# Mamba stage of a four-layer chain: three state buffers, softplus and first products moved, norm rows and residual on ScalarE and GpSimd

## The chip, the cores and the metric

The kernel runs on one core of a Trainium2 chip. The metric is the time of one execution in device microseconds; a median over runs is given. The engines are TensorE (PE in the rows, PEld is its weight load), VectorE (DVE), ScalarE (ACT), GpSimd (POOL) and SyncE (SP), which issues all transfers here.

## The reference

Four blocks follow one another on x of shape (4, 512, 256), in float32: two cross-attention blocks, a Mamba block and a last attention block. Only the Mamba block (the middle stage) is touched. It works on sequences of 64 context rows followed by 512 rows, for 4 batches, in 4 layers:

```python
def mamba_block(x, ip_w, cw, cb, xp_w, dtp_w, dtp_b, A_log, Dp, op_w):
    xz = jnp.einsum('bsd,ed->bse', x, ip_w)
    xi, z = jnp.split(xz, 2, axis=-1)
    ...
    xi = jax.nn.silu(conv.transpose(0, 2, 1))
    xdbl = jnp.einsum('bse,fe->bsf', xi, xp_w)
    dt, Bm, Cm = jnp.split(xdbl, [DR_, DR_ + DS_], axis=-1)
    dt = jax.nn.softplus(jnp.einsum('bsr,er->bse', dt, dtp_w) + dtp_b)
    A = -jnp.exp(A_log)
    dA = jnp.exp(dt[..., None] * A)
    dBu = dt[..., None] * Bm[:, :, None, :] * xi[..., None]
    ...            # h = dA * h + dBu ; y = sum over states of h * C
    y = ys.transpose(1, 0, 2) + xi * Dp
    y = y * jax.nn.silu(z)
    return jnp.einsum('bse,de->bsd', y, op_w)
...
h = h + mamba_block(rmsnorm(h, norm_w[l]), ...)    # for each of 4 layers
```

The inner width is 512, there are 16 states, a convolution over 4 rows, and rmsnorm is x * rsqrt(mean(x*x) + eps) * w.

## The kernel before, in words

The Mamba stage holds everything feature-major: 128 features by columns, where the columns are the 4 batches of 576 rows laid end to end. They are cut into five chunks (`CHUNKS`) of 384, 512, 512, 512 and 384 columns. One chunk of one layer is an item, `g` from 0 to 19; items 0, 5, 10, 15 are the first of a layer and 4, 9, 14, 19 the last (`last_of`).

An item is 64 units: 16 states `n` by 4 feature tiles `e`, numbered `q = 4n + e`. In each unit ScalarE computes a decay exp(dt*A) into one of three PSUM banks (L1800, `decay`, two units ahead of the scan), GpSimd multiplies u by the B row into one of four buffers `db` (L2052, `state_input`, three units ahead), and VectorE runs the recurrence as one scan instruction (L2004) into the state buffer `hh`, of which there are two, picked by `n % 2`. After the four scans of a state TensorE transposes them in tiles of 128 rows (`turn`, L1729). Of a 512-wide item two of the four tiles go to bank 5 (`TURN_D`), where VectorE multiplies each with its C column and adds it to `yt` (L2018; for state 0 a plain product, L2014). The other two go to bank 6 (`TURN_P`), where ScalarE scales them into `ys` (`scaled`, L1812) and TensorE adds them up with an identity product (`add`, L1739). ScalarE also keeps the last column of each state for the next item (`keep`, L1821), and a scan into a state buffer waits for the `keep` and the last turn of the state that was in it.

Between the units stand the side jobs of the two neighbouring items (`side`): those of the item before, `post` (back-turn of y, gating, output product, residual into `h`), and those that prepare the next, `pre` (norm, input products, convolution, x and dt products, softplus, gate z). At which unit each stands is set by a table of numbers:

```python
VAR, IN, YF, CONV, XD = 1, (6, 8, 10, 12), (14, 16, 18, 20), (22, 25, 28, 31), 34
DTP, BCT, SOFT, OUT, Z = 37, 44, 45, (58, 61), (46, 49, 52, 55)
```

The numbers are the units at which TensorE does its part; ScalarE and VectorE follow one to three units later. Every engine takes its instructions strictly in this written order. All side products go through a single PSUM bank, 7 (`SIDES`), so each waits until the one before it has been emptied. So at the start of an item (q = 0) ScalarE squares h (L1847); at q = 2 it turns the mean into rstd with a logarithm and an exponential (L1852, L1855), each of which is preceded by a table load; at q = 4 and 5 VectorE makes the normed rows `xn` (L1962); and from q = 6 TensorE makes the input products from them, which ScalarE copies into `xc` (L1862) and SyncE writes to memory for the convolution. VectorE adds the two halves of the output product to `h` at q = 60 and 63 (L1948).

## Time and profile before

| | |
|---|---|
| median of 3 runs | 4411.18 us (4409.15 to 4416.01) |
| the profiled execution's own time | 4420.25 us |
| its span in the trace | 4418.1 us |
| busy, of the span: TensorE, VectorE, ScalarE, GpSimd | 85%, 69%, 53%, 48% |
| Mamba stage, first to last scan | 1501 to 3590 us, 2089 us |

Busy shares of the whole span mix stages; the Mamba stage is read by itself. In the rows below, consecutive instructions of one engine overlap by some 0.09 us: two scans in a row are given as 2.45 us while one is 1.27 us, so the step from start to start is what an instruction costs.

### The profile page before, as it was taken

How to read it: one execution, taken by the hardware profiler on the slowest of the kernel's cores; microseconds unless marked ns; L12 is line 12 of the kernel's file. 1: busy time of each engine (PE TensorE's matmuls, PEld its weight loads, DVE VectorE, ACT ScalarE, POOL GpSimd, SP SyncE). 2: the span in 40 equal slices, each digit the busy share in tenths (PEclk: the TensorE clock that was granted, in tenths of full speed). 3: DMA queues.
4: the chain of work that ended last, by engine and by line, in shares of the span. 5: the costliest groups of instructions: out<-in, count | busy, mean ns of one | idle time of the engine just before them, and what ended most of it. 6: DMA issues, size and time to landing. Idle time of an engine off the chain costs nothing. (4 is left out here: it accounts for less than half of the span.)

```text
span 4418.1 us, 51543 instructions
## 1 busy us (share of the span) xinstructions
PE 3755.0 (85%) x16536; PEld 1943.5 (44%) x16536; DVE 3056.4 (69%) x4176; ACT 2354.4 (53%) x4473; POOL 2114.1 (48%) x2144
## 2 busy tenths in 40 slices
PE   8999999999988688888888888887888768888787
PEld 4444444444444244444444444444444434344443
DVE  4426435364353499999999999999999956474653
ACT  2334323233231477767777677776777626354462
POOL 1003112031120378877888877787788833132230
PEclk9999999999999799999999999999999979999999
DMA  3110000000000533223332233322432120000000
GB/s 147 39 57 1 1 19 1 10 10 1 15 1 0 150 84 87 75 81 94 91 87 72 78 94 87 86 83 78 112 87 80 46 79 1 11 1 11 1 6 5
DMA packets 135961, 228.47 MB, mean 52 GB/s; under 512 B 19280, under 2 KB 118864, under 8 KB 126864
## 3 DMA queue, kind: packets, MB, share of 16 engines
q1 hardware_dynamic: 135696, 225.20, 17.3%
q8 instruction: 135, 2.21, 0.2%
q14 instruction: 130, 1.06, 0.1%
HBM read 192.55 MB, written 32.60 MB: 51 GB/s over the span
## 5 line engine op out<-in xcount | busy, mean ns | idle before, releaser
L2052 POOL TENSOR_TENSOR m_db<-m_u,m_bb 128x512 f32<-128x512 f32 (+1 forms) x1280 | 1466.1, 1165 | 418.6 <-DVE m_hh L2004 415.4
L2004 DVE TENSOR_TENSOR_SCAN m_hh<-psum,m_kept,m_db 128x512 f32<-128x512 f32 (+1 forms) x1024 | 1196.2, 1202 | 29.9 <-ACT m_kept L1821 23.3
L1800 ACT ACTIVATE psum<-m_dt,m_am 128x512 f32<-128x512 f32 (+1 forms) x1280 | 817.7, 644 | 394.2 <-DVE m_hh L2004 390.6
L1729 PE MATMUL psum<-cst,m_hh 128*128 128x128 f32 x4608 | 659.7, 284 | 324.8 <-DVE m_yt L2018 227.6
L1729 PEld LDWEIGHTS psum<-cst,m_hh 128*128 128x128 f32 x4608 | 524.3, 144 | 753.4 <-DVE m_yt L2018 440.1
L1739 PE MATMUL psum<-m_ys,cst 128*128 128x512 f32 x1024 | 545.5, 615 | 0.0
L2018 DVE SCALAR_TENSOR_TENSOR m_yt<-psum,m_bc,m_yt 128x512 f32<-128x512 f32 x600 | 437.9, 730 | 41.1 <-PE psum L1729 40.0
L798 POOL TENSOR_SCALAR a_pr<-a_pr,a_ri 128x512 f32<-128x512 f32 x256 | 174.1, 694 | 609.5 <-DVE a_ri L612 609.5
L1812 ACT ACTIVATE m_ys<-psum,m_bc 128x512 f32<-128x512 f32 x512 | 344.7, 673 | 25.5 <-PE psum L1729 24.0
L798 POOL TENSOR_SCALAR c_pr<-c_pr,c_ri 128x512 f32<-128x512 f32 x256 | 172.5, 694 | 364.6 <-DVE c_ri L731 364.6
L652 ACT ACTIVATE a_pr<-psum,a_mx 128x512 f32<-128x512 f32 x256 | 173.7, 684 | 268.2 <-DVE a_mx L602 268.2
L1615 PE MATMUL psum<-m_xn,m_wa 128*128 128x512 f32 (+1 forms) x640 | 296.7, 591 | 3.9 <-DVE m_xn L1962 3.6
L2004 DVE TENSOR_TENSOR_SCAN m_hh<-psum,m_db 128x384 f32<-128x384 f32 x256 | 232.4, 941 | 19.9 <-ACT m_kept L1821 11.7
L602 DVE TENSOR_REDUCE a_mx<-psum 128x2 f32<-128x1024 f32 x128 | 155.9, 1220 | 130.4 <-PE psum L552 130.4
L1739 PEld LDWEIGHTS psum<-m_ys,cst 128*128 128x128 f32 x1024 | 170.0, 196 | 97.6 <-issue 71.7
L723 DVE TENSOR_REDUCE c_mx<-psum 128x1 f32<-128x512 f32 x256 | 164.0, 683 | 59.3 <-PE psum L679 59.3
L787 ACT ACTIVATE c_pr<-psum,c_mx 128x512 f32<-128x512 f32 x256 | 173.3, 684 | 49.9 <-DVE c_mx L723 48.7
L532 POOL TENSOR_TENSOR a_pr<-a_pr,a_ri 128x512 f32<-128x512 f32 x32 | 33.3, 1042 | 292.6 <-DVE a_ri L498 292.6
L688 PE MATMUL psum<-cst,c_pr 128*128 128x128 f32 x1024 | 156.4, 288 | 19.8 <-ACT c_ptr L773 15.3
L562 PE MATMUL psum<-cst,a_pr 128*128 128x128 f32 x1024 | 153.2, 284 | 18.2 <-POOL a_pr L798 15.9
L562 PEld LDWEIGHTS psum<-cst,a_pr 128*128 128x128 f32 x1024 | 111.4, 143 | 128.4 <-DVE a_slots L635 64.5
L635 DVE COPY a_slots<-psum 128x512 f32<-128x512 f32 x256 | 162.7, 676 | 6.8 <-PE psum L562 6.8
(242 smaller groups left out, 5624.2 us busy)
## 6 DMA issues: line engine op xcount, KB each, us to landing
m_bb<-b_rows SPq DMA_DIRECT2D x48, 1024.0 KB, 4.7
m_xr<-x_line SPq DMA_DIRECT2D x128, 192.0 KB, 4.0
m_bb<-b_rows SPq DMA_DIRECT2D x32, 768.0 KB, 4.5
m_xr<-x_line SPq DMA_DIRECT2D x128, 160.0 KB, 3.6
m_xr<-x_line SPq DMA_DIRECT2D x128, 128.0 KB, 3.3
m_xr<-x_line SPq DMA_DIRECT2D x128, 96.0 KB, 3.5
x_line<-m_xc SPq DMA_DIRECT2D x32, 192.0 KB, 2.8
m_wa<-w_in SPq DMA_DIRECT2D x4, 1376.0 KB, 7.4
```

The source lines that it names most:

```text
L562: mm = nc.tensor.transpose(b[:, kt * P:(kt + 1) * P], self.pr[:, u % 6, kt * P:(kt + 1) * P], ident)
L652: nc.scalar.activation(self.pr[:, u % 6, :], self.full(f"{name} s {u}"), ACT.Exp, bias=self.nm[:, u % 8:u % 8 + 1], accum_out=self.smh[:, ...
L787: nc.scalar.activation(self.pr[:, u % 6, :], self.full(f"{name} s {u}"), ACT.Exp, bias=self.nm[:, u % 8:u % 8 + 1], accum_out=self.smh[:, ...
L798: nc.gpsimd.tensor_scalar(self.pr[:, u % 6, :], self.pr[:, u % 6, :], self.rih[:, u % 8:u % 8 + 1], 1.0, ALU.mult, ALU.mult)\
L1615: mm = nc.tensor.matmul(full(job)[0:m, 0:w], lhs, rhs, start=k == 0, stop=k == n - 1)
L1729: mm = nc.tensor.transpose(s[:, e * P:(e + 1) * P], hh[:, n % 2, e, t * P:(t + 1) * P], ident)
L1739: nc.tensor.matmul(bank(SUMS[k]), ident, ys[:, k, :], start=n == 0, stop=n == LAST)\
L1800: nc.scalar.activation(bank(DECAY[u % len(DECAY)])[:, 0:w], dt[:, g % 2, e, 0:w], ACT.Exp, scale=am[:, layer_of(g) % 2, e * DS + n:e * DS ...
L1812: nc.scalar.activation(ys[:, k, :], bank(TURN_P), ACT.Identity, scale=bc[:, g % 2, t, DR + DS + n:DR + DS + n + 1], bias=0.0)\
L2004: nc.vector.tensor_tensor_scan(hh[:, n % 2, e, 0:w], bank(DECAY[u % len(DECAY)])[:, 0:w], db[:, u % 4, 0:w], kept[:, n, e:e + 1] if g % NI ...
L2018: nc.vector.scalar_tensor_tensor(y, bank(TURN_D), c, y, ALU.mult, ALU.add)\
L2052: nc.gpsimd.tensor_tensor(db[:, u % 4, 0:w], us[:, g % 2, e, 0:w], bb[:, at % 2, n % 4, 0:w], ALU.mult).then_inc(pool_done, pr.pool.step(f ...
```

## The change

It has seven parts.

1. `hh` gets three buffers, picked by `(16g + n) % 3`. To make room, `xc` now shares the memory of `yg`, and `sq` that of a new `res`, which brings new waits.
2. Softplus moves from unit 45 to 46; the gate products Z from 46, 49, 52, 55 to 47, 50, 53, 55; the products u on GpSimd from 50, 52, 54, 56 to 51, 53, 55, 57.
3. The first products of each item (state 0, two tiles) go from VectorE to ScalarE (`first`).
4. The normed rows: ScalarE multiplies h by the weight right after the squares (`weighted`, two instructions), and GpSimd multiplies that by rstd at q = 5 and 6; VectorE's two instructions are gone.
5. The input products move from 6, 8, 10, 12 to 7, 9, 11, 13.
6. The residual: ScalarE takes the output product out of PSUM, halved (`res`), and GpSimd adds it to `h`; VectorE's two instructions are gone. The output products move from 58, 61 to 57, 60.
7. The small vectors are loaded ahead of the weights, with a semaphore of their own (`vectors_loaded`).

```diff
@@ tables and buffers
-            hh = sb("hh", [P, 2, NE, BANK])
+            HH = 3
+            hh = sb("hh", [P, HH, NE, BANK])
+            rstd = sb("rstd", [P, BANK])
+            res = sb("res", [P, ND, BANK])
+            sq = res
             yg = sb("yg", [P, NE, BANK])
+            xc = yg
-            VAR, IN, YF, CONV, XD = 1, (6, 8, 10, 12), (14, 16, 18, 20), (22, 25, 28, 31), 34
-            DTP, BCT, SOFT, OUT, Z = 37, 44, 45, (58, 61), (46, 49, 52, 55)
+            VAR, IN, YF, CONV, XD = 1, (7, 9, 11, 13), (14, 16, 18, 20), (22, 25, 28, 31), 34
+            DTP, BCT, SOFT, OUT, Z = 37, 44, 46, (57, 60), (47, 50, 53, 55)
+            U, CUT = (51, 53, 55, 57), 58
@@ ScalarE
+                    def first(g, k):
+                        t = tiles_d(g)[k]
+                        if k == 0 and g >= 2:
+                            act.wait_ge(pe_done, pr.pe.at(f"{g - 2} yf {NE - 1}"))
+                        act.wait_ge(pe_done, pr.pe.at(f"{g} ht 0 {t}"))
+                        nc.scalar.activation(yt[:, g % 2, t, :], bank(TURN_D), ACT.Identity,
+                                             scale=bc[:, g % 2, t, DR + DS:DR + DS + 1], bias=0.0)\
+                            .then_inc(act_done, pr.act.step(f"{g} y 0 {t}"))
...
+                            for j in range(ND):
+                                if q == OUT[j] + 2:
+                                    if post:
+                                        act.wait_ge(pool_done, pr.pool.at(f"{post - 1} h {j}"))
+                                    act.wait_ge(pe_done, pr.pe.at(f"{post} out {j}"))
+                                    nc.scalar.activation(res[:, j, 0:width(post)], full(f"{post} out {j}")[:, 0:width(post)],
+                                                         ACT.Copy, scale=0.5).then_inc(act_done, pr.act.step(f"{post} res {j}"))
...
+                            if g >= 3:
+                                act.wait_ge(pool_done, pr.pool.at(f"{g - 3} h 1"))
                             for j in range(ND):
                                 nc.scalar.activation(sq[:, j, 0:w], h[:, j, at:at + w], ACT.Square)\
                                     .then_inc(act_done, pr.act.step(f"{g} squares" if j else None))
+                            act.wait_ge(vectors_loaded, 16 * (layer_of(g) + 1))
+                            for j in range(ND):
+                                nc.scalar.activation(xn[:, j, 0:w], h[:, j, at:at + w], ACT.Copy, scale=vec2(g, "norm", j))\
+                                    .then_inc(act_done, pr.act.step(f"{g} weighted" if j else None))
...
-                            nc.scalar.activation(s, s, ACT.Exp, scale=-0.5)\
+                            nc.scalar.activation(rstd[:, 0:w], s, ACT.Exp, scale=-0.5)\
                                 .then_inc(act_done, pr.act.step(f"{g} rstd"))
...
                             if before and e == 1:
+                                if before[1] == 0:
+                                    first(before[0], 0)
                                 scaled(*before, 0)
...
+                                if before[1] == 0:
+                                    first(before[0], 1)
@@ VectorE
+                                    if post + 2 < ITEMS:
+                                        dve.wait_ge(x_written[e % 2], written(post + 2, e))
                                     nc.vector.scalar_tensor_tensor(yg[:, e, 0:w], xi[:, post % 2, e, 0:w],
...
-                                if q == OUT[j] + 2:
-                                    dve.wait_ge(pe_done, pr.pe.at(f"{post} out {j}"))
-                                    nc.vector.scalar_tensor_tensor(h[:, j, at:at + w], full(f"{post} out {j}")[:, 0:w], 0.5,
...
-                            if q == VAR + 3 + k:
-                                dve.wait_ge(act_done, pr.act.at(f"{g} rstd"))
...
-                                nc.vector.scalar_tensor_tensor(xn[:, k, 0:w], h[:, k, at:at + w], vec2(g, "norm", k),
-                                                               full(f"{g} var")[:, 0:w], ALU.mult, ALU.mult)\
...
-                            if DS * g + n >= 2:
-                                i, m = divmod(DS * g + n - 2, DS)
+                            if DS * g + n >= HH:
+                                i, m = divmod(DS * g + n - HH, DS)
@@ GpSimd
+                                if q == OUT[j] + 3:
+                                    pool.wait_ge(act_done, pr.act.at(f"{post} res {j}"))
+                                    nc.gpsimd.tensor_tensor(h[:, j, at:at + w], h[:, j, at:at + w], res[:, j, 0:w], ALU.add)\
+                                        .then_inc(pool_done, pr.pool.step(f"{post} h {j}"))
...
+                            if q == VAR + 4 + k:
+                                pool.wait_ge(act_done, pr.act.at(f"{g} rstd"))
+                                nc.gpsimd.tensor_tensor(xn[:, k, 0:w], xn[:, k, 0:w], rstd[:, 0:w], ALU.mult)\
+                                    .then_inc(pool_done, pr.pool.step(f"{g} xn" if k else None))
```

ScalarE, around the start of item 12 (q = 63 of item 11 to q = 2), before: decay, the two squares, decay, scaled tile, decay, keep, then the logarithm and the exponential with their table loads.

```order
L1800 ACTIVATE psum<-m_dt,m_am 128x512
L1847 ACTIVATE m_sq<-m_h 128x512 x2
L1800 ACTIVATE psum<-m_dt,m_am 128x512
L1812 ACTIVATE m_ys<-psum,m_bc 128x512
L1800 ACTIVATE psum<-m_dt,m_am 128x512
L1821 ACTIVATE m_kept<-m_hh 128x4
L1852 ACT_TABLE_LOAD
L1852 ACTIVATE psum<-psum,m_eps 128x512
L1855 ACT_TABLE_LOAD
L1855 ACTIVATE psum<-psum 128x512
```

The same place of the change (the squares are written into `res`, L1874; the weighted rows are L1878, the residual copy L1856):

```order
L1856 ACTIVATE m_res<-psum 128x384
L1808 ACTIVATE psum<-m_dt,m_am 128x512
L1820 ACTIVATE m_ys<-psum,m_bc 128x512
L1808 ACTIVATE psum<-m_dt,m_am 128x512
L1874 ACTIVATE m_res<-m_h 128x512 x2
L1878 ACTIVATE m_xn<-m_h,m_va 128x512 x2
L1808 ACTIVATE psum<-m_dt,m_am 128x512
L1820 ACTIVATE m_ys<-psum,m_bc 128x512
L1808 ACTIVATE psum<-m_dt,m_am 128x512
L1839 ACTIVATE m_kept<-m_hh 128x4
L1883 ACT_TABLE_LOAD
L1883 ACTIVATE psum<-psum,m_eps 128x512
```

The second half of the residual copy stands three activations ahead of the squares, and two weighted rows now stand between the squares and the next decay.

ScalarE a little later (q = 4 to 6 of item 12), before, from the first `yp` copy (L1831) on:

```order
L1831 ACTIVATE m_yp<-psum 128x512
L1800 ACTIVATE psum<-m_dt,m_am 128x512
L1812 ACTIVATE m_ys<-psum,m_bc 128x512
L1800 ACTIVATE psum<-m_dt,m_am 128x512
L1821 ACTIVATE m_kept<-m_hh 128x4
```

And of the change, where the first product is L1830:

```order
L1849 ACTIVATE m_yp<-psum 128x512
L1808 ACTIVATE psum<-m_dt,m_am 128x512
L1830 ACTIVATE m_yt<-psum,m_bc 128x512
L1820 ACTIVATE m_ys<-psum,m_bc 128x512
L1808 ACTIVATE psum<-m_dt,m_am 128x512
L1839 ACTIVATE m_kept<-m_hh 128x4
```

The first product stands ahead of the scaled tile of state 0.

TensorE from the last gate product (`m_xn`, q = 55) to the last half of the output product (`m_yg`) in item 11, before; `m_hh` x8 are two turns of four transposes, `m_ys` the identity product of the sum:

```order
L1615 MATMUL psum<-m_xn,m_wa 128x512 x2
L1729 MATMUL psum<-cst,m_hh 128x128 x8
L1739 MATMUL psum<-m_ys,cst 128x512
L1729 MATMUL psum<-cst,m_hh 128x128 x8
L1615 MATMUL psum<-m_yg,m_wb 128x384 x2
L1739 MATMUL psum<-m_ys,cst 128x512
L1615 MATMUL psum<-m_yg,m_wb 128x384 x2
L1729 MATMUL psum<-cst,m_hh 128x128 x8
L1739 MATMUL psum<-m_ys,cst 128x512
L1615 MATMUL psum<-m_yg,m_wb 128x384 x2
L1729 MATMUL psum<-cst,m_hh 128x128 x8
L1615 MATMUL psum<-m_yg,m_wb 128x384 x2
```

And of the change:

```order
L1623 MATMUL psum<-m_xn,m_wa 128x512 x2
L1737 MATMUL psum<-cst,m_hh 128x128 x8
L1747 MATMUL psum<-m_ys,cst 128x512
L1623 MATMUL psum<-m_yg,m_wb 128x384 x2
L1737 MATMUL psum<-cst,m_hh 128x128 x8
L1623 MATMUL psum<-m_yg,m_wb 128x384 x2
L1747 MATMUL psum<-m_ys,cst 128x512
L1737 MATMUL psum<-cst,m_hh 128x128 x8
L1623 MATMUL psum<-m_yg,m_wb 128x384 x2
L1747 MATMUL psum<-m_ys,cst 128x512
L1623 MATMUL psum<-m_yg,m_wb 128x384 x2
L1737 MATMUL psum<-cst,m_hh 128x128 x8
```

The last half of the output product now stands ahead of the turns of q = 62, where it stood behind them.

## Rows read from the trace of the kernel before

**Rows 1.** The page, part 1: busy time of each engine, share of the span, instructions.
```profile
PE 3755.0 (85%) x16536; PEld 1943.5 (44%) x16536; DVE 3056.4 (69%) x4176; ACT 2354.4 (53%) x4473; POOL 2114.1 (48%) x2144
```

**Rows 2.** Windows: us, busy PE, PEld, DVE, ACT, POOL, PEclk; Mamba stage, then item 11.
```profile
1501.00:3590.00 2089.00, 1752.43 (x7889) 948.21 (x7887) 1975.55 (x2259) 1509.85 (x2648) 1647.45 (x1500) 0.96 0.30 84
2641.20:2753.20 112.00, 97.26 (x431) 51.85 (x430) 106.63 (x115) 83.20 (x143) 89.32 (x74) 0.95 0.31 90
```

**Rows 3.** Groups by line, 1501:3590, VectorE: xcount | busy us, mean ns | idle before.
```profile
L2004 DVE TENSOR_TENSOR_SCAN m_hh<-psum,m_kept,m_db 128x512 f32<-128x512 f32 (+1 forms) x1024 | 1196.2, 1202 | 29.9 <-ACT m_kept L1821 23.3 <-ACT psum L1800 5.1 <-POOL m_db L2052 1.4
...
L2018 DVE SCALAR_TENSOR_TENSOR m_yt<-psum,m_bc,m_yt 128x512 f32<-128x512 f32 x600 | 437.9, 730 | 41.1 <-PE psum L1729 40.0
...
L2014 DVE TENSOR_SCALAR m_yt<-psum,m_bc 128x512 f32<-128x512 f32 x40 | 29.1, 728 | 0.1
...
L1962 DVE SCALAR_TENSOR_TENSOR m_xn<-m_h,m_va,psum 128x512 f32<-128x512 f32 (+1 forms) x38 | 26.3, 692 | 6.0 <-ACT psum L1855 6.0
...
L1948 DVE SCALAR_TENSOR_TENSOR m_h<-psum,m_h 128x512 f32<-128x512 f32 (+1 forms) x38 | 24.2, 638 | 16.1 <-PE psum L1615 16.1
```

**Rows 4.** The same view, 1501:3590, GpSimd and ScalarE.
```profile
L2052 POOL TENSOR_TENSOR m_db<-m_u,m_bb 128x512 f32<-128x512 f32 (+1 forms) x1279 | 1465.1, 1165 | 418.6 <-DVE m_hh L2004 415.4 <-DVE m_cwr L1971 1.6 <-POOL m_db L2052 0.3
...
L1812 ACT ACTIVATE m_ys<-psum,m_bc 128x512 f32<-128x512 f32 x512 | 344.7, 673 | 25.5 <-PE psum L1729 24.0
```

**Rows 5.** Waits of VectorE, 1500:3750: us in total, times, longest.
```profile
DVE m_yt L2018 <- PE psum L1729: 40.0, 58, 2.3
DVE m_hh L2004 <- ACT m_kept L1821: 35.0, 16, 2.9
DVE m_h L1948 <- PE psum L1615: 26.4, 25, 7.9
```

**Rows 6.** Timeline of ScalarE, item 11, softplus: start, us, idle before in brackets.
```profile
2719.32 1.28 ACT L1892 ACT_TABLE_LOAD   x1
...
2723.84 0.69 ACT L1800 ACTIVATE psum<-m_dt,m_am 128x512 f32<-128x512 f32 x1
```

**Rows 7.** Timeline of VectorE, item 11, after the softplus.
```profile
2724.88 1.28 DVE L2004 TENSOR_TENSOR_SCAN m_hh<-psum,m_kept,m_db 128x512 f32<-128x512 f32 x1 [2.19 <-ACT m_kept L1821]
...
2728.80 2.45 DVE L2004 TENSOR_TENSOR_SCAN m_hh<-psum,m_kept,m_db 128x512 f32<-128x512 f32 x2
```

**Rows 8.** Timeline of TensorE, item 11, gate products to output products.
```profile
2727.25 3.57 PE L1615 MATMUL psum<-m_xn,m_wa 128*128 128x512 f32 x4
...
2737.92 1.98 PE L1615 MATMUL psum<-m_xn,m_wa 128*128 128x512 f32 x4
...
2750.86 1.46 PE L1615 MATMUL psum<-m_yg,m_wb 128*128 128x384 f32 x4
2752.15 1.02 PE L1739 MATMUL psum<-m_ys,cst 128*128 128x512 f32 x2
2753.01 1.04 PE L1729 MATMUL psum<-cst,m_hh 128*128 128x128 f32 x8
```

**Rows 9.** Timeline of ScalarE across the boundary from item 11 to item 12.
```profile
2752.88 1.14 ACT L1847 ACTIVATE m_sq<-m_h 128x512 f32<-128x512 f32 x2
2754.54 0.69 ACT L1800 ACTIVATE psum<-m_dt,m_am 128x512 f32<-128x512 f32 x1 [0.52 <-DVE m_hh L2004]
...
2756.57 1.28 ACT L1852 ACT_TABLE_LOAD   x1
...
2760.33 0.69 ACT L1800 ACTIVATE psum<-m_dt,m_am 128x512 f32<-128x512 f32 x1
...
2763.21 0.69 ACT L1812 ACTIVATE m_ys<-psum,m_bc 128x512 f32<-128x512 f32 x1
```

**Rows 10.** Timeline of TensorE, first units of item 12.
```profile
2761.67 1.11 PE L1729 MATMUL psum<-cst,m_hh 128*128 128x128 f32 x4 [1.62 <-ACT m_ys L1812]
...
2765.44 1.88 PE L1615 MATMUL psum<-m_xn,m_wa 128*128 128x512 f32 x4
```

**Rows 11.** Timeline of VectorE, item 12, tenth and eleventh unit.
```profile
2772.54 0.75 DVE L2018 SCALAR_TENSOR_TENSOR m_yt<-psum,m_bc,m_yt 128x512 f32<-128x512 f32 x1 [0.46 <-PE psum L1729]
```

More of the change, by code:

```diff
@@ L1440, in build @@
             h = sb("h", [P, ND, B * S2])
-            xc = sb("xc", [P, NE, BANK])
             xr = sb("xr", [P, 2, 4, BANK])
@@ L1921, in _ @@
                                 keep(*before)
-                            if before and e == 3 and len(tiles_p(before[0])) > 1:
-                                scaled(*before, 1)
+                            if before and e == 3:
+                                if len(tiles_p(before[0])) > 1:
+                                    scaled(*before, 1)
+                                if before[1] == 0:
+                                    first(before[0], 1)
                             side(NE * n + e, *neighbours(g))
@@ L2101, in prepare @@
                             rates(layer_of(g))
-                        if q == SOFT + 12 and border(g) is not None:
+                        if q == CUT and border(g) is not None:
                             b = border(g)
```

68 lines of the change are left out of this document (34 added, 34 removed).

## The prediction

> **What bounds the kernel now.** The page comes first, for the shares of the whole span [rows 1]. They mix four stages, and the change touches one, so the next view is the windows: in the Mamba stage VectorE is busy 1975.6 of 2089 us, GpSimd 1647, ScalarE 1510, TensorE 1752 [rows 2]. That says VectorE, and the waits agree: GpSimd's and ScalarE's largest idle is until a scan is done [rows 4], while VectorE's own waits are short. But 113 us of VectorE's stage are idle, and who ends these waits decides what less VectorE work is worth: TensorE's turns 40 us, ScalarE's `keep` 35 us, the output product 26 us [rows 5]. So the third view is the timeline of one item, read by units q. There VectorE is not alone on the path: TensorE is busy 97.3 of item 11's 112.0 us [rows 2], and around the start of an item ScalarE's chain of squares, logarithm, exponential and two table loads runs with all of its two-unit lead used up.
>
> **VectorE's side of the sum.** It loses 40 first products of 0.73 us, 38 normed rows of 0.69 and 38 residual additions of 0.64 [rows 3], busy 79.6 us. One instruction costs its length less an overlap of about 0.09 us (a pair of scans is 2.45 us long, one is 1.28 [rows 7]), so 116 of them free about 79.6 - 10 = 70 us. Beside it stand waits that could go: 35 us at `keep` and 26 us at the output product [rows 5]. If all of it came through, the kernel would be about 70 + 50 = 120 us faster. I don't think so, for what follows; the working is for item 11 and the start of item 12, whose rows are typical (the stage repeats itself by layers).
>
> **Softplus.** ScalarE starts its table load at 2719.32 and issues the next decay at 2723.84 [rows 6], 4.52 us, over twice its lead. VectorE waits 2.19 us, by the row for `keep` [rows 7]. A third state buffer takes the `keep` out of it, but that decay lasts until 2724.53, 0.35 us before the scan starts: alone it is worth 0.3 us. One unit later, softplus has one more decay ahead of it. The block ends 0.7 us later (a decay of 0.61 and a `keep`), and the scan that waits is the next one, at about 2724.95; with one gate row (0.58) then still to be done, the scan of unit 50 starts near 2727.7 instead of 2728.80 [rows 7]. After the second gate row the lead is 1.65 us. Call it 1.1 to 1.7 us an item.
>
> **From the gate to the output product.** What becomes of this lead is TensorE's to say. All side products pass through bank 7. The last gate product stays at unit 55, and it needs the gate row before it, which VectorE did at unit 54 and now does at 55, behind one more scan and one more addition (1.18 + 0.65 us). So the lead of 1.65 us is used up and the product starts at 2738.0, as before [rows 8]. Behind it TensorE has, in written order, this product 1.72, two turns 0.87 three times, the sum 0.86 three times, and four half output products of 1.29 each from start to start [rows 8]: 1.72 + 2.61 + 2.58 + 5.16 = 12.1 us, so the last half ends at 2750.1 where it ended at 2752.15. VectorE no longer waits for it (0.61 + 0.5 us twice at the wide ones, 0.46 at the narrow ones), but the turns of unit 62 now stand behind it and come 0.9 us later. Gain at the end of the item: about 1.9 us.
>
> **The start of the next item.** This is where I expect it to go. ScalarE takes the residual out of PSUM (0.5 us, to 2750.65), then come decay, scaled tile, decay (0.61 + 0.57 + 0.61) and the squares can start at 2752.5, against 2752.88 [rows 9]; GpSimd's addition, which they also wait for, is ready by then (a product is 1.17 us [rows 4]). Two weighted rows follow, priced as the two squares, 1.06 us. Of these 0.52 are covered, since the decay behind them waits that long for a scan today [rows 9]. So the logarithm starts 1.06 - 0.52 - 0.4 = 0.1 to 0.2 us later than now. From its table load to the next decay are 3.76 us (2756.57 to 2760.33 [rows 9]), and today scan 5 starts as that decay ends: the normed row that leaves VectorE there was filler, and so are most of the next three removed instructions, because the decays of units 5 to 9 come one by one behind it. Then the first product (0.57 us, priced as the scaled tile, 0.67 long [rows 4]) stands ahead of the scaled tile of state 0, which TensorE waits for (1.62 us for the one before it [rows 10]). Some 0.4 us of that is absorbed, for TensorE today starts the next turns 0.4 us after the tile is ready. The first input product thus comes 0.3 to 0.5 us later than at 2765.44 [rows 10], and from there to unit 15 TensorE has no idle time: a product 1.72, a sum 0.86 and two turns 0.87 are 3.45 us for two units, and VectorE needs 3.0. It waits for the turns already today (0.46 us at 2772.54 [rows 11]). VectorE's freed 2.6 us at an item's start become waiting, and the item of 112 us comes out 0.4 us longer, not 4 us shorter.
>
> The moved input products change no total, for in both orders each stands between the same two pairs of turns. GpSimd gets four products more an item, 1.24 us each at full width (1.17 over the stage [rows 4]): 76 x 1.17 = 89 us of the 440 that it idles; worked through units 51 to 63, it has made up the delay by unit 63.
>
> **The other boundaries and the sum.** Per layer of five items: two boundaries as above, +0.4 each. Three carry a 512-wide output product, which today costs two waits of 0.51 us that go, against 1.7 us more for TensorE; and two of these prepare a 384-wide item, behind whose start no wait for a turn stands and VectorE is still the bound, so that part of its freed time counts: I put these at +0.5, -0.8 and -1.2. Together 0.8 - 1.5 = -0.7 us a layer, -3 us in all. Outside the boundaries: the last item loses its two first products (1.3 us) and some wait at the output product, the lead-in and the tail gain a GpSimd product and an addition each behind ScalarE (about +1 twice): nothing together. The profiled execution took 4420.25 us (span 4418.1), 0.2% above the median of the runs, 4411.18. So 4417 in such an execution, and 4408 as median.
>
> **A rule against moving work to GpSimd.** GpSimd's products keep a mean of 1.17 us over a stage in which VectorE is busy 95% of the time [rows 2, 4], and a scan, which reads PSUM and one buffer, takes 1.28 beside them [rows 7]; by this the moved products cost nobody more. The Trainium skill, SBUF — State Buffer (the section with the single rule on ports), says that GpSimd shares a port pair with VectorE as an exclusive lock when VectorE reads two SBUF inputs or runs in a two-port mode. No VectorE instruction of this stage's steady part reads two SBUF tiles, so by that rule too the sum stays. Its page Perfetto Trace Analysis (Optimizing Scalar/DVE Operations) advises to offload a saturated VectorE to ScalarE; by that advice the freed time would count, which is the first rival.
>
> **Rivals.** (a) VectorE's time does count. For: it is busy 95% of the stage. Against: scan 5 and the turns wait for others. If each of the 19 boundaries keeps half of the 2.6 us freed at its start and half of the softplus lead, that is 1.3 + 0.8 - 0.4 = 1.7 us, 32 us: 4379. In full, 4291; I give that almost nothing. (b) Slower: ScalarE's chain at the item's start is longer than I price it. The place is between the residual copy and the logarithm: if the squares start 1 us later than in my working (the copy waits for TensorE, GpSimd's addition behind it), all 19 boundaries are 1.5 us longer, 28 us: 4439. It decides as soon as squares start over 0.5 us later than today. TensorE adds to it: after idling it runs slowly for a few us (the same four matmuls took 3.57 us after a wait and 1.98 otherwise [rows 8]), and its wait at the start grows from 1.6 + 1.1 to about 3.3 us. (c) GpSimd becomes late: u products, residual and normed rows within 20 units are ten products of 1.24 against a slack of 0.27 us a unit and four buffers; if two units of it showed, 2.5 us an item, 45 us: 4456. (d) The shared memory of `xc` and `yg` makes VectorE wait for SyncE's writes at unit 15; a write has seven units to land. Unlikely.
>
> **How the numbers follow.** 0.2% (9 us) is about what a measurement can tell from no change. My case, the freed time is taken back: 0.40, by itself 4395 to 4425, of which 0.12 is over 0.2% faster, 0.23 within and 0.05 slower. (a) 0.28, faster. (b) 0.24, of which 0.02 within. (c) and (d) 0.08, slower. Faster 0.40, same 0.25, slower 0.35. The unknown prices bound it: all weighted rows and first products covered (-1.6 us a boundary, -30) and none covered (+30). 4370 to 4442 leaves out the full gain and the full GpSimd delay.
>
> **What would show it.** Right: VectorE's busy time in the stage down by 80 us and its idle up by as much; its largest waits on ScalarE's decay (L1808) near units 5 to 9 and on turns; `keep` gone from its waits; softplus wait near 0 to 1 us; squares of item 13 within 0.5 us of where they stand now relative to the item's start. Wrong: VectorE's idle stays near 113 us (then rival a), or the logarithm starts more than a microsecond later in the item (b), or scans wait for `db` (c).

## The result and the profile after

The changed kernel takes 4441.62 us (median of 4 runs, 4439.5 to 4442.1), the kernel before beside it 4412.95 us (4 runs). The ratio of the runs is 1.0059 with the interval [1.0046, 1.0071], which is 26 us; the two medians are 28.7 us apart. So the change made the kernel slower. The forecast was 4408 us; rival (b), a longer chain of ScalarE at the start of an item, had been given 4439 us and a chance of 0.24.

VectorE did lose the work. The page, part 1, of the changed kernel, against [rows 1]:

```profile
PE 3752.0 (84%) x16536; PEld 1939.5 (44%) x16536; DVE 2991.0 (67%) x4056; ACT 2408.0 (54%) x4593; POOL 2202.9 (50%) x2224
```

The windows view of the Mamba stage, in the columns of [rows 2]:

```profile
1501.00:3620.00 2119.00, 1761.42 (x7901) 953.28 (x7900) 1907.85 (x2139) 1558.16 (x2760) 1729.73 (x1574) 0.96 0.29 82
```

VectorE is busy 1907.9 us instead of 1975.6 and idle 211 us instead of 113. 68 us of work went and 98 us of idle time came; the difference is the window, which is 30 us longer. From the first scan to the last the stage is 23.0 us longer in the two profiled executions, whose spans differ by 22.2 us (4440.3 against 4418.1); the kernel before was profiled in an execution 7 us above its median of these runs.

The waits of VectorE and then of TensorE in the changed kernel, 1500:3625, us in total, times, longest, against [rows 5]:

```profile
DVE m_yt L2045 <- PE psum L1737: 110.7, 105, 4.0
DVE m_hh L2030 <- ACT psum L1808: 77.2, 57, 3.0
...
PE psum L1737 <- DVE m_yt L2045: 182.4, 168, 3.4
PE psum L1737 <- ACT m_ys L1820: 113.8, 91, 5.6
PE psum L1737 <- ACT m_yt L1830: 18.2, 5, 4.7
```

Two lines of the same view of the kernel before, which [rows 5] do not have:

```profile
DVE m_hh L2004 <- ACT psum L1800: 5.1, 3, 1.7
PE psum L1729 <- ACT m_ys L1812: 82.1, 78, 2.9
```

The waits for `keep` (35.0 us) and for the output product (26.4 us) are gone from VectorE's list, the second because VectorE no longer has that instruction. In their place it waits 110.7 us for turns, before 40.0, and 77.2 us for ScalarE's decays, before 5.1. TensorE's own waits for ScalarE say what is behind the turns: 113.8 us for the scaled tile (82.1 before) and 18.2 us for the first product.

### The profile page after: what moved, and what is told of

Same layout as the page of the kernel before. It is cut to its first block and busy times, and to the rows that moved or that the text cites. A ratio compares the mean times of both kernels' runs of the same rounds, so it can differ in the third digit from the quotient of the medians.

```text
span 4440.3 us, 51731 instructions
## 1 busy us (share of the span) xinstructions
PE 3752.0 (84%) x16536; PEld 1939.5 (44%) x16536; DVE 2991.0 (67%) x4056; ACT 2408.0 (54%) x4593; POOL 2202.9 (50%) x2224
## 5 line engine op out<-in xcount | busy, mean ns | idle before, releaser
L1747 PE MATMUL psum<-m_ys,cst 128*128 128x512 f32 x1024 | 554.5, 624 | 0.0
L2045 DVE SCALAR_TENSOR_TENSOR m_yt<-psum,m_bc,m_yt 128x512 f32<-128x512 f32 x600 | 439.1, 732 | 113.2 <-PE psum L1737 110.7
L1623 PE MATMUL psum<-m_xn,m_wa 128*128 128x512 f32 (+1 forms) x640 | 294.8, 588 | 18.5 <-DVE m_zs L2008 13.9
L1623 PEld LDWEIGHTS psum<-m_xn,m_wa 128*128 128x128 f32 x640 | 127.8, 207 | 157.9 <-issue 98.5
L1747 PEld LDWEIGHTS psum<-m_ys,cst 128*128 128x128 f32 x1024 | 165.1, 198 | 62.1 <-issue 43.0
```

The source lines that it names most:

```text
L1623: mm = nc.tensor.matmul(full(job)[0:m, 0:w], lhs, rhs, start=k == 0, stop=k == n - 1)
L1747: nc.tensor.matmul(bank(SUMS[k]), ident, ys[:, k, :], start=n == 0, stop=n == LAST)\
L2045: nc.vector.scalar_tensor_tensor(y, bank(TURN_D), c, y, ALU.mult, ALU.add)\
```

## Where the time went in an item

Two instants mark a boundary: the scan of unit 44 of an item and that of the next item. Their distance, changed minus before, for the five kinds of boundary of a layer (from item 0 to 1, 1 to 2, and so on, the last into the next layer), in us. The first row gives the prediction's five terms in the order of the kinds:

```
boundary            0>1   1>2   2>3   3>4   4>0'
forecast           +0.4  +0.4  +0.5  -0.8  -1.2
layer 1            +1.8  +1.1  +1.0  -1.1  +2.3
layer 2            +2.9  +1.0  +1.3  -0.6  +1.7
layer 3            +3.5  +1.0  +1.3  -0.6  +1.9
layer 4            +4.5  +4.1  +3.7  -1.1
```

The 19 boundaries add 29.6 us. The first 44 units (-2.7) and what follows unit 44 of the last item (-4.0) bring that to 23.0.

The scans also say where in an item the loss arises. Counted from unit 44 and added up over the 19 boundaries, the changed kernel is 1.8 us ahead at unit 8 of the next item and 32.7 us behind at unit 10. Between these two units stands VectorE's first addition that waits for TensorE behind the first input product. What ScalarE's chain delays thus reaches VectorE by way of TensorE.

**From item 11 to 12 (kind 1>2), the one worked in the prediction.** The scan of unit 44 of item 11 starts at 2716.33 before and at 2724.74 after, so times of the changed kernel are compared less 8.41 us. Its timeline of ScalarE (start, us, idle before in brackets):

```profile
2759.39 0.49 ACT L1856 ACTIVATE m_res<-psum 128x384 f32<-128x384 f32 x1 [2.05 <-PE psum L1623]
...
2761.57 1.14 ACT L1874 ACTIVATE m_res<-m_h 128x512 f32<-128x512 f32 x2
2762.61 1.32 ACT L1878 ACTIVATE m_xn<-m_h,m_va 128x512 f32<-128x512 f32 x2
2763.84 0.67 ACT L1808 ACTIVATE psum<-m_dt,m_am 128x512 f32<-128x512 f32 x1
...
2765.85 1.28 ACT L1883 ACT_TABLE_LOAD   x1
2767.14 0.66 ACT L1883 ACTIVATE psum<-psum,m_eps 128x512 f32<-128x512 f32 x1
```

The residual copy waits 2.05 us at the head of ScalarE's queue for the output product, and the decays behind it wait with it. The squares start at 2753.16 on the clock of before, 0.28 us later than in [rows 9]; the working had them 0.38 earlier. The two weighted rows take 1.23 us from start to start (priced 1.06). The logarithm's table load is 0.87 us later than in [rows 9], not 0.1 to 0.2. Behind it, on VectorE:

```profile
2733.68 1.28 DVE L2030 TENSOR_TENSOR_SCAN m_hh<-psum,m_kept,m_db 128x512 f32<-128x512 f32 x1 [1.39 <-ACT psum L1808]
...
2736.11 2.45 DVE L2030 TENSOR_TENSOR_SCAN m_hh<-psum,m_kept,m_db 128x512 f32<-128x512 f32 x2
...
2770.33 3.65 DVE L2030 TENSOR_TENSOR_SCAN m_hh<-psum,m_kept,m_db 128x512 f32<-128x512 f32 x3 [2.09 <-ACT psum L1808]
...
2778.08 0.75 DVE L2045 SCALAR_TENSOR_TENSOR m_yt<-psum,m_bc,m_yt 128x512 f32<-128x512 f32 x1 [1.22 <-PE psum L1737]
```

The first two rows are the softplus: the wait is one scan later and 1.39 us, and the scan of unit 50 starts at 2736.11 - 8.41 = 2727.70, where the prediction put 2727.7. The last two are the new waits at the item's start, 2.09 us for the decay behind the exponential and 1.22 for the turn, which stands behind the first input product. The boundary is 1.0 us longer.

**From item 10 to 11 (kind 0>1), which was not worked.** Here item 10 has units of 384, and the scan of its unit 44 is 4.93 us later than before (2609.99, 2614.92). ScalarE before, then after:

```profile
2640.89 1.13 ACT L1847 ACTIVATE m_sq<-m_h 128x512 f32<-128x512 f32 x2
...
2644.59 1.28 ACT L1852 ACT_TABLE_LOAD   x1
```

```profile
2644.93 0.49 ACT L1856 ACTIVATE m_res<-psum 128x384 f32<-128x384 f32 x1 [1.19 <-PE psum L1623]
2645.32 1.30 ACT L1808 ACTIVATE psum<-m_dt,m_am 128x512 f32<-128x512 f32 x2
2647.30 1.15 ACT L1874 ACTIVATE m_res<-m_h 128x512 f32<-128x512 f32 x2 [0.68 <-PE psum L1737]
2648.35 1.32 ACT L1878 ACTIVATE m_xn<-m_h,m_va 128x512 f32<-128x512 f32 x2
...
2651.59 1.28 ACT L1883 ACT_TABLE_LOAD   x1
```

The squares are 6.41 - 4.93 = 1.48 us later in the item, the logarithm 7.00 - 4.93 = 2.07. The view names TensorE for the 0.68 us before the squares, but the program makes them wait for GpSimd's residual addition too, because squares and residual now share one buffer, and GpSimd's timeline shows that addition ending last:

```profile
2642.46 3.77 POOL L2079 TENSOR_TENSOR m_db<-m_u,m_bb 128x512 f32<-128x512 f32 x3
2646.16 1.02 POOL L2116 TENSOR_TENSOR m_h<-m_h,m_res 128x384 f32<-128x384 f32 x1
```

It ran from 2646.16 to 2647.18, behind three state products. Over the whole stage the waits view names this addition five times as what ended the wait of the squares:

```profile
ACT m_res L1874 <- POOL m_h L2116: 5.7, 5, 2.1
```

Then TensorE, before and after:

```profile
2651.40 1.97 PE L1729 MATMUL psum<-cst,m_hh 128*128 128x128 f32 x8 [2.90 <-ACT m_ys L1812]
2653.16 3.11 PE L1615 MATMUL psum<-m_xn,m_wa 128*128 128x512 f32 x4
```

```profile
2658.97 1.97 PE L1737 MATMUL psum<-cst,m_hh 128*128 128x128 f32 x8 [5.56 <-ACT m_ys L1820]
2660.73 1.92 PE L1747 MATMUL psum<-m_ys,cst 128*128 128x512 f32 x2
2662.44 3.10 PE L1623 MATMUL psum<-m_xn,m_wa 128*128 128x512 f32 x4
```

It idles 5.56 us instead of 2.90. A slow stretch was there before as well, but the sum (L1747) now falls into it too: 1.92 us, where the same two matmuls take 1.02 a few units later. The windows view of the changed kernel has the granted clock at 0.50 there, which is 1.2 GHz, after the 5.56 us of idle time:

```profile
2659.00:2662.00 3.00, 3.00 (x10) 2.41 (x11) 3.00 (x3) 2.89 (x6) 3.00 (x3) 0.50 0.00 0
```

VectorE's addition behind it waits 3.96 us where it waited 0.51, before and after:

```profile
2657.60 0.75 DVE L2018 SCALAR_TENSOR_TENSOR m_yt<-psum,m_bc,m_yt 128x512 f32<-128x512 f32 x1 [0.51 <-PE psum L1729]
```

```profile
2666.01 0.75 DVE L2045 SCALAR_TENSOR_TENSOR m_yt<-psum,m_bc,m_yt 128x512 f32<-128x512 f32 x1 [3.96 <-PE psum L1737]
```

That boundary is 3.5 us longer.

**From item 14 to 15 (kind 4>0'), which was to gain.** Item 15 has units of 384. Its start on VectorE, before and after:

```profile
3084.14 0.75 DVE L2018 SCALAR_TENSOR_TENSOR m_yt<-psum,m_bc,m_yt 128x512 f32<-128x512 f32 x1 [0.77 <-PE psum L1729]
```

```profile
3087.42 2.65 DVE L2030 TENSOR_TENSOR_SCAN m_hh<-psum,m_db 128x384 f32<-128x384 f32 x3 [2.98 <-ACT psum L1808]
...
3095.91 0.75 DVE L2045 SCALAR_TENSOR_TENSOR m_yt<-psum,m_bc,m_yt 128x512 f32<-128x512 f32 x1 [3.53 <-PE psum L1737]
```

So VectorE waits for a decay and for a turn here as well; it is not the bound. For the turn it waited 0.77 us already before.

**The same chain, another price.** The boundary from item 16 to 17 is of the same kind as that from 11 to 12, but 4.1 us longer instead of 1.0. Up to unit 8 the scans of items 12 and 17 run alike (unit 8 starts 13.52 us behind unit 0 in both), and unit 10 comes 2.35 us later in item 17. There TensorE works at half the clock. The first input product of item 12, then that of item 17 with its window:

```profile
2775.73 1.88 PE L1623 MATMUL psum<-m_xn,m_wa 128*128 128x512 f32 x4
```

```profile
3308.42 2.67 PE L1623 MATMUL psum<-m_xn,m_wa 128*128 128x512 f32 x4
```

```profile
3305.00:3309.00 4.00, 4.00 (x11) 2.73 (x12) 2.58 (x3) 3.44 (x7) 4.00 (x5) 0.50 0.00 0
```

What a boundary costs thus depends on the chain and on which products the slow stretch meets. Before unit 0 the two boundaries differ by the rest, 0.7 us.

## The experiments

The code cuts show the lines that take effect; where a whole table of units would stand, only the entries that change may be given. Four theories are told apart. A: ScalarE's chain at the start of an item (squares, weighted rows, logarithm, exponential, first product) became longer and sets the time. B: the hand-offs over GpSimd (residual, normed rows) are late. C: the moved units and shared buffers cost. D: any work given to ScalarE costs, wherever it stands. Ratios are to the kernel before, run on the same chip; differences between ratios are put in us of the kernel before.

**First products back on VectorE.** In the changed kernel:

```
-                        if n == 0:
-                            return
                         dve.wait_ge(pe_done, pr.pe.at(f"{g} ht {n} {t}"))
+                        if n == 0:
+                            nc.vector.tensor_scalar(y, bank(TURN_D), c, None, ALU.mult)\
+                                .then_inc(dve_done, pr.dve.step(f"{g} y {n} {t}"))
+                            return
```

> The changed kernel with one part undone: the first products of each item (state 0) are VectorE's again. Theory A (ScalarE's chain at the item's start holds TensorE, whose slow products follow): the scaled tile of state 0 comes 0.57 us earlier at each of 19 boundaries and TensorE's wait shrinks by as much: 10 to 20 us faster than the changed kernel, near 4425, and VectorE's wait for turns well under 110 us. Theory B (the loss is in GpSimd's hand-offs: residual addition and normed rows): no change, 4438 to 4445. Theory C (the moved units and the shared buffers cost it): no change either, or 26 us slower, as VectorE has 40 x 0.65 us more.

Measured 4436.59 us, ratio 1.0042 [1.0027, 1.0057]. Against 1.0059 that is 0.0017, 7.5 us, for 40 instructions. The two intervals overlap, so the step is not clear of noise, and it is smaller than the 10 to 20 us that A had promised.

**Normed rows back on VectorE**, with the input products at units 6, 8, 10, 12 again:

```
-                            for j in range(ND):
-                                nc.scalar.activation(xn[:, j, 0:w], h[:, j, at:at + w], ACT.Copy, scale=vec2(g, "norm", j))
...
+                            if q == VAR + 3 + k:
+                                nc.vector.scalar_tensor_tensor(xn[:, k, 0:w], h[:, k, at:at + w], vec2(g, "norm", k),
+                                                               full(f"{g} var")[:, 0:w], ALU.mult, ALU.mult)
```

> The changed kernel with the normed rows back on VectorE, as before, and the input products back at units 6, 8, 10, 12. ScalarE has no weighted rows, GpSimd no products for them. Theory A: the logarithm starts 0.7 to 1.2 us earlier at each boundary: 15 to 30 us faster than the changed kernel, 4412 to 4427. Theory B: faster too, but the log's start moves little and GpSimd's waits go instead; 5 to 10 us. Theory C: 0 to 5 us.

Measured 4425.26 us, 1.0017 [1.0007, 1.0026]: 0.0042 less than the changed kernel, 18.5 us, the largest of the three and within what A had promised (15 to 30). VectorE's waits for the decay fell with it:

```profile
DVE m_yt L2078 <- PE psum L1744: 101.2, 101, 3.6
DVE m_hh L2059 <- ACT psum L1815: 28.7, 24, 2.4
```

**Residual back on VectorE**, output products at 58 and 61 again:

```
-                                    nc.scalar.activation(res[:, j, 0:width(post)], full(f"{post} out {j}")[:, 0:width(post)],
-                                                         ACT.Copy, scale=0.5)
-                                    nc.gpsimd.tensor_tensor(h[:, j, at:at + w], h[:, j, at:at + w], res[:, j, 0:w], ALU.add)
+                                    nc.vector.scalar_tensor_tensor(h[:, j, at:at + w], full(f"{post} out {j}")[:, 0:w], 0.5,
+                                                                   h[:, j, at:at + w], ALU.mult, ALU.add)
...
-            OUT = (57, 60)
+            OUT = (58, 61)
```

> The changed kernel with the residual back on VectorE and the output products back at units 58 and 61. Theory A: ScalarE's wait for the output product (74 us in all) goes from its chain, the squares start earlier by up to 1 us where the output is 512 wide; VectorE gets 1.2 us an item and its waits of 0.5 us back: between 5 us faster and 10 us slower than the changed kernel. Theory B (GpSimd's addition is what the squares wait for): 10 to 20 us faster. Theory C (the output product ahead of the turns of unit 62 costs 2.5 us an item): about 15 us faster.

Measured 4433.28 us, 1.0036 [1.0024, 1.0048]: 0.0023, 10 us, with intervals that overlap by a little. This is more than A allowed (5 us faster at most) and the lower edge of B's 10 to 20. It does not say whether ScalarE's wait for the output product or GpSimd's addition behind it is what costs.

**All three back**, which leaves three buffers and the moved softplus and gate products; against the kernel before:

```
-            DTP, BCT, SOFT, OUT, Z = 37, 44, 45, (58, 61), (46, 49, 52, 55)
+            DTP, BCT, SOFT, OUT, Z = 37, 44, 46, (58, 61), (47, 50, 53, 55)
```

> Three state buffers, softplus at unit 46 and the gate products at 47, 50, 53, 55 alone, with the shared buffers; first products, normed rows and residual are VectorE's as before, and units 6 to 12 and 58, 61 as before. Theory A: it keeps the gain of the softplus stretch (3.8 us a layer in the changed kernel's trace, 35 us of waits at keep before) and none of the loss: 12 to 30 us faster than the kernel before, 4383 to 4401. Theory C: no faster than the kernel before, 4410 to 4425.

Measured 4411.97 us, 0.999 [0.9981, 0.9999]. So the three moves together cost 0.0069, 30 us, and one by one 0.0082: no single one is the culprit, and their costs about add. What is left of the change costs nothing on balance, so C is not the cause of the loss. But it gains only 4 us and not the 12 to 30 that A had promised for it; the time lies where C had put it (4410 to 4425), and a run below finds the moved unit that takes the gain back.

**Weighted rows off the chain**, in the changed kernel:

```
+                        if q == 57 and g + 1 < ITEMS and (g + 1) % NI:
+                            weighted(g + 1)
...
+                            if g % NI == 0:
+                                weighted(g)
```

> The changed kernel with the two weighted rows of an item made at unit 57 of the item before it (for the first item of a layer they stay where they are): the same work on the same engine, off the stretch between squares and logarithm. Theory A (ScalarE's chain at the item's start): 1.2 us earlier at 15 of 19 boundaries, 12 to 20 us faster than the changed kernel, 1.0015 to 1.0035 times the kernel before. Theory D (it is how much ScalarE has to do in all, or GpSimd's products behind it, that costs): no change, 1.005 to 1.007.

Measured 4422.04 us, 1.0019 [1.0008, 1.0029]: 0.0040, 17.6 us, with the same work on every engine. So for these rows it is the place in ScalarE's queue that costs, not the amount: D fell as the cause of the loss. The profile is less clean than the time, and it is of an execution of 4433.2 us, among the slowest of ten (4417 to 4434.6). In layers 2 and 3 its boundaries are as long as in the changed kernel (6.8 and 6.5 us over before, against 6.3 and 7.1). At the boundary from item 10 to 11 the squares come 2.6 us later in the item than before, and the view names GpSimd's residual addition for it, which is a mark of B:

```profile
2646.78 1.15 ACT L1890 ACTIVATE m_res<-m_h 128x512 f32<-128x512 f32 x2 [1.13 <-POOL m_h L2130]
```

The gain is in layers 1 and 4 (-1.2 and +0.6 us, against +5.1 and +11.2), and why these differ is open.

**The logarithm left out of the changed kernel, and of the kernel before**, two kernels with one edit:

```
-                            nc.scalar.activation(s, s, ACT.Ln, bias=eps2[:, 0:1])\
-                                .then_inc(act_done, pr.act.step(f"{g} log"))
-                            act.wait_ge(act_done, pr.act.n)
```

> The changed kernel with the logarithm left out (rstd is then exp(-0.5 var), so the norm computes something else; the table load in front of each of the two goes too): ScalarE's chain at an item's start is 1.3 + 0.7 + up to 1.3 = 2 to 3.2 us shorter and nothing else changes. Theory A: all of it comes through, for that chain is the path: 38 to 60 us faster than the changed kernel, 0.992 to 0.997 of the kernel before. Theory D: 10 to 20 us.

> The kernel before with the same left out. Theory A as I put it in the prediction (the chain was already the path there, with VectorE's removed work as filler in its shadow): faster, but less than the changed kernel gains, as VectorE becomes the bound within 1 to 1.5 us: 15 to 35 us, 0.992 to 0.9965. Theory A' (it was VectorE that bound the start, and the chain only became the path by the added instructions): under 8 us, above 0.998.

Measured 4390.25 us, 0.9947 [0.993, 0.9963], and 4400.38 us, 0.9966 [0.9955, 0.9977]. One edit takes 51 us from the changed kernel and 15 us from the kernel before. It shortens the chain by two table loads and the logarithm, 1.28 + 1.28 + 0.66 = 3.2 us; at 19 places that is 61 us, of which 51 show after and 15 before. This is the clearest reading of A: before, three quarters of that length were covered by other work, after the change a sixth. That it was VectorE's own work that covered it is the prediction's argument; no run shows it apart. The mean granted clock is 0.966 in both profiled executions, against 0.960 (changed) and 0.959 (before) with the logarithm, so a part of both gains may be the clock's; it rose alike in both, so the difference between them is hardly the clock's. VectorE's waits without the logarithm, of the changed kernel:

```profile
DVE m_yt L2042 <- PE psum L1737: 97.2, 101, 4.3
DVE m_hh L2027 <- ACT psum L1808: 30.5, 27, 2.4
```

It also says what the whole change is worth with the chain made this much shorter: 4400.38 - 4390.25 = 10 us, of the 70 that VectorE had given up. Most of them are still waits for turns.

**Gate products at 47, 49, 52, 55 with all three pieces back:**

```
-            DTP, BCT, SOFT, OUT, Z = 37, 44, 46, (58, 61), (47, 50, 53, 55)
+            DTP, BCT, SOFT, OUT, Z = 37, 44, 46, (58, 61), (47, 49, 52, 55)
```

> The run with softplus and three buffers alone, with the gate products at 47, 49, 52, 55 instead of 47, 50, 53, 55. There the last gate product waits for a gate row at unit 55; here that row is at 54, as in the kernel before. Theory A: units 53 to 63 lose the 1.0 us an item that they are longer than before: 10 to 20 us faster than that run, 0.9955 to 0.998 of the kernel before. Rival (VectorE's wait for softplus is only moved and TensorE's order does not matter): 0.999 as it was.

Measured 4399.05 us, 0.9966 [0.9953, 0.9979], faster than both kernels and 13 us below the run with all three back. With 47, 50, 53, 55 the last gate product still waited for its gate row, as the prediction says; TensorE before this edit and, in the second fence, after it:

```profile
2732.78 1.99 PE L1627 MATMUL psum<-m_xn,m_wa 128*128 128x512 f32 x4 [1.03 <-DVE m_zs L2037]
```

```profile
2726.32 1.98 PE L1627 MATMUL psum<-m_xn,m_wa 128*128 128x512 f32 x4
```

The wait of 1.03 us is gone. The clock changed with it: this kernel's executions have a mean granted clock of 0.964 to 0.967, those of the run with 47, 50, 53, 55 have 0.959 to 0.962. How the 13 us divide between the wait and the clock was not separated. At the boundary from item 11 to 12 this kernel is granted the full clock; the windows of 24 us around it, of the kernel before and of this one:

```profile
2745.00:2769.00 24.00, 21.31 (x91) 12.91 (x91) 24.00 (x27) 19.83 (x34) 18.19 (x15) 0.93 0.12 47
```

```profile
2733.00:2757.00 24.00, 20.54 (x93) 12.29 (x92) 24.00 (x26) 20.35 (x35) 19.04 (x17) 1.00 0.12 49
```

**The same with two state buffers** (HH = 3 becomes HH = 2):

> Kernel before with softplus one unit later and gate products at units 47, 49, 52, 55, but two state buffers as before. The same with three buffers took 4399.05 us, 16 less than the kernel before beside it. Theory 'the third buffer matters': with two, the wait for the copied last columns (keep) is back in VectorE's waits, some 15 to 35 us of it, and the time returns to 4408 to 4420. Theory 'the order of the units matters': the move takes the decay out of softplus' way by itself, and the time stays at 4397 to 4405, keep's waits under 10 us.

Measured 4401.17 us, 0.9971 [0.9959, 0.9982]. So the time stays, and the third buffer is not needed for it. The order of the units alone takes the `keep` out of VectorE's waits; the wait behind softplus is the 1.39 us of the changed kernel, for the decay:

```profile
1672.03 1.28 DVE L2059 TENSOR_TENSOR_SCAN m_hh<-psum,m_kept,m_db 128x512 f32<-128x512 f32 x1 [1.39 <-ACT psum L1815]
```

**Three buffers and nothing moved**, against the 4399 us kernel:

```
-            DTP, BCT, SOFT, OUT, Z = 37, 44, 46, (58, 61), (47, 49, 52, 55)
-            U, CUT = (51, 53, 55, 57), 58
+            DTP, BCT, SOFT, OUT, Z = 37, 44, 45, (58, 61), (46, 49, 52, 55)
+            U, CUT = (50, 52, 54, 56), 57
```

> Kernel before with a third state buffer and nothing moved (softplus 45, gates 46, 49, 52, 55). Theory 'the third buffer matters': keep's 35 us of waits go and most of that shows, 4395 to 4403. Theory 'the order of the units matters' (the prediction's: alone worth 0.3 us an item, 16 items): the wait goes over to the decay behind softplus, some 30 us of VectorE's waits on ScalarE's decays, and the time is 4408 to 4413.

Measured 4415.01 us against 4415.79, 1.0 [0.999, 1.001]. This kernel also has the shared buffers and the early load of the small vectors, so these bring and cost nothing that can be told either. The 35 us of waits for `keep` are 35 us of waits for the decay behind it:

```profile
DVE m_yt L2078 <- PE psum L1744: 35.5, 56, 2.1
DVE m_hh L2059 <- ACT psum L1815: 35.3, 19, 2.7
```

**The 4399 us kernel with the weighted rows at unit 57 and their product on GpSimd:**

```
+                        if q == 57 and g + 1 < ITEMS and (g + 1) % NI:
+                            weighted(g + 1)
...
+                                nc.gpsimd.tensor_tensor(xn[:, k, 0:w], xn[:, k, 0:w], rstd[:, 0:w], ALU.mult)\
...
-            VAR, IN, YF, CONV, XD = 1, (6, 8, 10, 12), (14, 16, 18, 20), (22, 25, 28, 31), 34
+            VAR, IN, YF, CONV, XD = 1, (7, 9, 11, 13), (14, 16, 18, 20), (22, 25, 28, 31), 34
```

> The 4399 us version (third buffer, softplus 46, gates 47, 49, 52, 55) with one more piece of the change: normed rows as weighted rows on ScalarE, done at unit 57 of the item before, and their product on GpSimd; input products at 7, 9, 11, 13. Theory A (ScalarE's chain at the item's start is what costs; VectorE's time is worth something once that chain is not longer): 4388 to 4398, the logarithm no later than in the 4399 us version. Rival D (any work given to ScalarE or GpSimd around a boundary costs, wherever it stands, and the freed VectorE time counts nothing): 4402 to 4412, by the input products that come one unit later and by 1.2 us of ScalarE per item.

Measured 4401.55 us, 0.997 [0.9959, 0.9981], between A's forecast (4388 to 4398) and D's (4402 to 4412), and nearer to D's. Kept off the chain, the 38 normed rows cost nothing; taken from VectorE, they bring nothing that these runs can tell, the part of D that held (its waits for turns and decays are 51.5 and 43.0 us, in the 4399 us kernel 44.4 and 27.2).

**The changed kernel with gates at 47, 49, 52, 55:**

> The changed kernel with gate products at 47, 49, 52, 55 in place of 47, 50, 53, 55 and nothing else. The same step in the version without the three moved pieces of work was worth 13 us. Theory 'costs of the two places add' (C beside A): 4441 - 13 = 4425 to 4432. Rival 'the item's start decides and the end's lead is lost in it' (A alone): 4436 to 4441, the scan of unit 0 earlier but units 0 to 16 longer by as much.

Measured 4444.23 us, 1.0065 [1.005, 1.008], above both forecasts (C beside A: 4425 to 4432; A alone: 4436 to 4441). The step that brought 13 us there brings nothing here, although the granted clock is higher (0.963 to 0.965, the changed kernel 0.958 to 0.961). In item 11 the second gate product is caught in a slow stretch, and the first output product waits again:

```profile
2743.36 3.15 PE L1623 MATMUL psum<-m_xn,m_wa 128*128 128x512 f32 x4
...
2759.13 1.53 PE L1623 MATMUL psum<-m_yg,m_wb 128*128 128x384 f32 x4 [1.68 <-DVE m_zs L2008]
```

In the changed kernel that gate product took 1.88 us. So the order of the gate products is no cost that stands beside A in the changed kernel. Nor is a higher clock by itself a gain.

## Why the prediction was wrong

**What bounds the kernel now: right.** VectorE's busy share was no measure of what its work is worth. Of 70 us freed, none arrived in the changed kernel.

**VectorE's side of the sum: right** in size: busy time in the stage down by 67.7 us, foreseen 70 net of overlaps. (The waits beside it are 35 + 26 = 61 us and were counted as 50; the full gain was given almost no chance, so nothing hangs on it.)

**Softplus: right**, to 0.1 us (scan of unit 50 at 2727.70, foreseen 2727.7), and so was that the third buffer alone is worth next to nothing. That the wait for `keep` goes without it was not seen.

**From the gate to the output product: right in mechanism, 0.6 us short.** The last gate product starts at 2746.47 - 8.41 = 2738.06 (foreseen 2738.0). The last output half starts at 2757.84 and takes 1.29, so it ends at 2750.7 on the clock of before, not 2750.1.

**The start of the next item: right in mechanism, mis-sized.** Foreseen +0.4 us, measured +1.0. The logarithm is 0.7 us later than foreseen. The squares give 0.66 of it (0.6 from the late output product, behind which the residual copy blocks ScalarE) and the weighted rows 0.17; what covers part of them was slightly more than the 0.52 counted. That GpSimd's addition "is ready by then" held at this boundary and not at that from item 10 to 11.

**The other boundaries and the sum: this is the step that failed.** The prediction worked one boundary, carried its +0.4 us over to kind 0>1, and let the boundaries into a 384-wide item gain, since behind such a start "no wait for a turn stands and VectorE is still the bound". The runs show otherwise. In item 15, which is 384 wide, VectorE waits 2.98 us for a decay and 3.53 us for a turn, and 0.77 us for that turn already before. Measured are +1.8 to +4.5 us where +0.4 stood for 0>1, +1.7 to +2.3 where -1.2 stood, and +29.6 us over all 19 where -3 stood. At the boundary from item 10 to 11 the squares waited for GpSimd besides, and TensorE idled 5.56 us instead of 2.90. In layer 4 two more boundaries are about 4 us longer (+4.1, +3.7); for the first of them the half clock at the first input product accounts for 2.35 us. Why the slow stretches fall otherwise there is open.

Kind 3>4 came out near its term (-0.6 to -1.1 against -0.8), but by luck. In layers 1 to 3 it is 0.5 to 1.0 us longer up to unit 36 of the narrow item, and then 1.6 us come back in one place, where a slow stretch of TensorE moved away from the x product (four matmuls in 2.79 us before, 1.49 after); in item 14, VectorE before and after:

```profile
3030.54 0.75 DVE L2018 SCALAR_TENSOR_TENSOR m_yt<-psum,m_bc,m_yt 128x512 f32<-128x512 f32 x1 [2.06 <-PE psum L1729]
```

```profile
3040.62 0.75 DVE L2045 SCALAR_TENSOR_TENSOR m_yt<-psum,m_bc,m_yt 128x512 f32<-128x512 f32 x1 [0.46 <-PE psum L1737]
```

In layer 4 the last item prepares no next one, so its -1.1 says nothing of the chain.

**Rival (b) is what happened**, in place and sign. Its size was met as a mean (1.5 us a boundary were given, 29.6 / 19 = 1.6 are measured), in part by luck, for single boundaries lie between -1.1 and +4.5. Its trigger, squares over 0.5 us later, holds at the boundary from item 10 to 11 (1.48) and not at the next (0.28), where late squares and weighted rows together made the logarithm late. Over the 18 boundaries that prepare an item, the squares are over 0.5 us later in 12, counted from unit 44. Rival (a) is refuted by VectorE's idle time in the windows, (c) by the waits: `db` is not among those of VectorE. GpSimd's share in (b) is small where the changed kernel's trace names it, 5.7 us in five waits of the squares and the 0.68 us at item 11; what these cost in the end was not separated from ScalarE's part, since no kernel gave the residual a buffer of its own. The Trainium skill, Perfetto Trace Analysis (Optimizing Scalar/DVE Operations), says that with a saturated VectorE it may make sense to offload some work to ScalarE or even GpSimd, which is less than the advice that the prediction made of it. In these runs it did not pay (1.0059), because the receiving engine was on the path just where the work was put.

## What to carry to other kernels

Before work is moved off the busiest engine, look at the receiving engine's place in the program, not at its total: a queue that works in order, has a dependent chain there and is waited for, can pay for nearly all of it (51 of 61 us here), and a copy that waits for another engine makes all behind it wait. Take a piece out of the suspected chain in both kernels (here the logarithm: 15 us before, 51 us after); the two answers say how much of the chain is covered. And a boundary worked out for one width is no price for the others. Before a place is let gain because nothing waits there, read its rows: here a wait of 0.77 us for a turn stood in the trace before, at the start of the narrow item.

## What the runs showed of the hardware

A table load takes 1.28 us and the activation behind it starts 0.01 us after its end (2765.85, 2767.14). The slow stretches of TensorE shown here come behind waits (5.56 us in item 11) and move with the order of the units: the second gate product of item 11, four matmuls, takes 3.57 us in the kernel before [rows 8], 1.88 in the changed one and 3.15 in the changed one with its gate products moved. The granted clock is 0.50 in them (2659 to 2662 and 3305 to 3309 us) and 1.00 in the boundary window of the 4399 us kernel. The mean over the whole span is 0.964 in the profiled execution of the 4399 us kernel and 0.960 in that of three buffers with nothing moved.

The fastest orders without a change in the work (0.964 to 0.966) are those with a higher granted clock, and the changed kernel's stays at 0.960. But the slowest kernel of all, the changed one with its gate products moved, has 0.963, so the mean clock does not rank the kernels; how much of the 16 us between these two kernels is the clock's was not measured apart from the waits.
